# Linear attention: the third output tile moves from VectorE to ScalarE and GpSimd

## The reference, cut to what matters

```python
sq = elu_plus_one(q)                      # phi of the queries
sk = elu_plus_one(k)
kv = jnp.einsum('bhsd,bhse->bhde', sk, v)
qkv = jnp.einsum('bhsd,bhde->bhse', sq, kv)
k_sum = sk.sum(axis=2)
norm = jnp.einsum('bhsd,bhd->bhs', sq, k_sum)
attn = qkv / (norm[..., None] + EPS)
attn = attn.transpose(0, 2, 1, 3).reshape(b, s, H * D)
return attn @ Wo.T
...
x = x + _L0_attn_ref(_layernorm(x, axis=-1), ...)
```

## Time and profile before

| what | us |
|---|---|
| median of 3 runs | 3445.62 |
| lowest and highest | 3444.78, 3446.63 |
| the profiled execution | 3444.01 |
| its span | 3442.3 |

### The profile page before, as it was taken

The page is one execution under the profiler, slowest core; times in us unless marked ns, Lnnn a source line. Parts: engine busy times, 40 slices in busy tenths (PEclk is TensorE's granted clock), DMA queues, the critical chain, the costliest instruction groups (busy, mean ns, idle before and its releaser), DMA issues.

```text
span 3442.3 us, 53010 instructions
## 1 busy us (share of the span) xinstructions
PE 3337.5 (97%) x19523; PEld 2854.1 (83%) x19526; DVE 2670.2 (78%) x5148; ACT 2042.7 (59%) x3733; POOL 1062.4 (31%) x1295
## 2 busy tenths in 40 slices
PE   6899999999999999999999999999999999999997
PEld 4778888778888888888888888888888888888885
DVE  6899996778877788867788677886788767876776
ACT  4777777665556565555555656556555565556553
POOL 4887767622122122122121312212212121212112
PEclk9999999999999999999999999999999999999999
DMA  2221212200000000000000110001000010001000
GB/s 86 88 77 54 64 58 82 64 16 13 13 25 25 13 13 13 13 25 25 13 15 15 28 44 16 13 15 27 22 15 15 16 32 25 16 19 29 28 18 22
DMA packets 98528, 104.24 MB, mean 30 GB/s; under 512 B 10336, under 2 KB 88800, under 8 KB 98144
## 3 DMA queue, kind: packets, MB, share of 16 engines
q1 hardware_dynamic: 98272, 100.85, 9.8%
HBM read 87.18 MB, written 13.63 MB: 29 GB/s over the span
## 4 chain that ended last, share of the span: by engine, by line
PE 72%; DVE 5%; ACT 3%; DMA 0%; issue 0%; POOL 0%; DVEq 0%; ACTq 0%; POOLq 0%; SPq 0%
PE at_ps_job L2021 12%; PE at_ps_job L35 7%; PE at_ps_job L37 7%; PE at_ps_job L36 7%; PE at_ps_o L35 6%; PE at_ps_o L37 6%; PE at_ps_o L36 6%; PE at_ps_s L35 6%; PE at_ps_s L36 6%; PE at_ps_s L37 6%; DVE at_neg_max L1948 1%; ACT x_resident L1772 1%; DVE at_probT_lo L1815 1%; PE at_ps_job L656 1%; DVE li_wkv_lo L1846 0%; ACT at_probT_hi L1731 0%
## 5 line engine op out<-in xcount | busy, mean ns | idle before, releaser
L1731 ACT ACTIVATE at_probT_hi<-at_ps_job 128x512 fp32r<-128x512 f32 x1024 | 611.7, 598 | 888.3 <-PE at_ps_job L2021 885.7
L1815 DVE TENSOR_TENSOR at_probT_lo<-at_ps_job,at_probT_hi 128x512 fp32r<-128x512 f32 x1024 | 703.4, 687 | 272.7 <-ACT at_probT_hi L1731 262.4
L1772 ACT ACTIVATE x_resident<-at_ps_s,at_neg_max 128x1024 f32<-128x1024 f32 x512 | 570.9, 1115 | 150.6 <-DVE at_neg_max L1948 145.8
L1706 POOL TENSOR_TENSOR li_wkv_hi<-li_bkv,ch_cols 128x256 fp32r<-128x256 f32 x252 | 154.9, 615 | 1607.3 <-PE at_ps_job L37 1556.9
L1948 DVE TENSOR_REDUCE at_neg_max<-at_ps_s 128x1 f32<-128x1024 f32 x512 | 622.6, 1216 | 5.2
L2021 PE MATMUL at_ps_job<-ident,x_resident 128*128 128x128 f32 x4096 | 613.7, 272 | 4.7 <-DVE at_probT_lo L1815 2.9
L2021 PEld LDWEIGHTS at_ps_job<-ident,x_resident 128*128 128x128 f32 x4096 | 496.0, 140 | 97.4 <-issue 7.3
L35 PE MATMUL at_ps_o<-at_probT_hi,at_v_lo 128*128 128x512 f32 x1024 | 446.3, 436 | 7.6 <-DVE li_wkv_lo L1846 6.6
L35 PE MATMUL at_ps_s<-at_k_hi,at_q_lo 128*128 128x512 f32 x1024 | 445.1, 435 | 0.0
L37 PE MATMUL at_ps_o<-at_probT_lo,at_v_hi 128*128 128x512 f32 x1024 | 404.4, 395 | 0.0
L36 PE MATMUL at_ps_s<-at_k_hi,at_q_hi 128*128 128x512 f32 x1024 | 402.1, 393 | 0.0
(11 more groups left out here) (356 smaller groups left out, 7444.3 us busy)
## 6 DMA issues: line engine op xcount, KB each, us to landing
li_bkv<-attn_w SPq DMA_DIRECT2D x256, 128.0 KB, 2.3
li_bkv<-mlp_w SPq DMA_DIRECT2D x112, 128.0 KB, 2.3
li_wo_hi<-li_wo_kept SPq DMA_DIRECT2D x24, 256.0 KB, 2.7
li_wo_lo<-li_wo_kept SPq DMA_DIRECT2D x24, 256.0 KB, 3.0
li_wq_hi<-li_wq_kept SPq DMA_DIRECT2D x48, 128.0 KB, 2.1
li_wq_lo<-li_wq_kept SPq DMA_DIRECT2D x48, 128.0 KB, 2.3
x_resident<-x SPq DMA_DIRECT2D x4, 1024.0 KB, 14.3
out<-x_resident SPq DMA_DIRECT2D x4, 1024.0 KB, 4.9
```

Source lines behind the costliest of these rows:

```text
L1706: nc.gpsimd.tensor_tensor(hi, src, none, ALU.add).then_inc(s_wh[part], 1)
L1731: nc.scalar.activation(ph[:, i // TC, 4 * half:4 * half + 4, (i % TC) * P:(i % TC + 1) * P], c.turned_bank(2 * TB * u + 2 * i + half), ACT ...
L1772: nc.scalar.activation(prob[:, slot % 2, :], ps_s[slot % 2][:], ACT.Exp, bias=nmax[:, slot:slot + 1], accum_out=rsum[:, u % 2, slot:slot + ...
L1815: nc.vector.tensor_tensor(pl[at], c.turned_bank(2 * TB * u + 2 * i + half), ph[at].bitcast(F32), ALU.subtract).then_inc(s_pl, 1)
```

## The change

Each unit's third tile goes the way of the fourth. VectorE does two of the four tiles instead of three. ScalarE scales two tiles, one after the other, into two neighbouring parts of `ybuf`. GpSimd adds both to x in one operation of 512 columns instead of one of 256, and waits for both. The list of bank releases, and the three semaphore counts, follow.

```diff
@@ step_claims
-        for j in range(3):
-            yield ("OUT", m, j), "x", 3 * m + j + 1
-        yield ("OUT", m, 3), "y3", m + 1
+        for j in range(2):
+            yield ("OUT", m, j), "x", 2 * m + j + 1
+        for j in range(2):
+            yield ("OUT", m, 2 + j), "y23", 2 * m + j + 1
...
-        ybuf = sb("ybuf", [P, 2, D], F32)
+        ybuf = sb("ybuf", [P, 2, 2, D], F32)
...
@@ gpsimd
-                    pool.wait_ge(s_y3, m + 1)
-                    x = x_tile_of(m, 3)
-                    nc.gpsimd.tensor_tensor(x, ybuf[:, m % 2, :], x, ALU.add).then_inc(s_x3, 1)
+                    pool.wait_ge(s_y3, 2 * m + 2)
+                    x = x_tile_of(m, slice(2, 4))
+                    nc.gpsimd.tensor_tensor(x, ybuf[:, m % 2], x, ALU.add).then_inc(s_x3, 1)
...
@@ scalar
-                    nc.scalar.activation(ybuf[:, m % 2, :], c.own_bank(("OUT", m, 3))[:, 0:D], ACT.Copy,
-                                         scale=rnorm[:, m % 2, 3:4]).then_inc(s_y3, 1)
+                    for j in range(2):
+                        nc.scalar.activation(ybuf[:, m % 2, j, :], c.own_bank(("OUT", m, 2 + j))[:, 0:D], ACT.Copy,
+                                             scale=rnorm[:, m % 2, 2 + j:3 + j]).then_inc(s_y3, 1)
...
@@ vector
-                        dve.wait_ge(s_y3, m - 1)
-                        dve.wait_ge(s_x, 3 * m - 3)
+                        dve.wait_ge(s_y3, 2 * m - 2)
+                        dve.wait_ge(s_x, 2 * m - 2)
...
-                    for j in range(3):
+                    for j in range(2):
                         x = x_tile_of(m, j)
                         nc.vector.scalar_tensor_tensor(x, c.own_bank(("OUT", m, j))[:, 0:D], rnorm[:, m % 2, j:j + 1], x, ALU.mult, ALU.add).then_inc(s_x, 1)
```

More of the change, by code:

```diff
@@ L1019, in linear_attention_phase @@
         aw = AttentionWeights(kv)
-        c.own_emptied = {"phi": s_f, "x": s_x, "y3": s_y3}
+        c.own_emptied = {"phi": s_f, "x": s_x, "y23": s_y3}
         block = ctx.enter_context(nc.Block())
@@ L1038, in x_tile_of @@
         def x_tile_of(m, j):
-            return sh.x[:, m // LOOP * TB + m % 2 * TC + j, :]
+            x = sh.x[:, m // LOOP * TB + m % 2 * TC:m // LOOP * TB + m % 2 * TC + TC, :]
+            return x[:, j, :]
         def ready(dve, kind, b):
@@ L1046, in ready @@
             if kind == "QB":
-                dve.wait_ge(s_x, 3 * LOOP)
+                dve.wait_ge(s_x, 2 * LOOP)
                 dve.wait_ge(s_x3, LOOP)
```

## The result

| | median us | lowest, highest | profiled span |
|---|---|---|---|
| before | 3445.2 | 3444.72, 3446.63 | 3442.3 |
| after | 3476.3 | 3474.48, 3479.55 | 3475.4 |

The ratio after to before is 1.0091, with a 95% interval of 1.0080 to 1.0103: 31 us slower, where 8.8 us faster was forecast and 3449 was the end of the range.

A forecast was written before the change was run, and what follows sets the result against it. Linear attention was taken as bound by VectorE's list in some stretches and TensorE in the others. Terms -12.7 - 2.5 + 3.0 + 2.5 + 0.9 = -8.8 us, forecast 3436.8 us (profiled 3435.2); range 3426 to 3449.

The forecast's parts named there:

- Where the time is bound: Linear attention: VectorE's list bounds some stretches, TensorE the others; 30.8 us of TensorE's stalls end with VectorE's `f`.
- Relief, -12.7: VectorE in linear attention: one tile fewer, net 0.30 us a step where VectorE is late; -12.7 us, bounds -30.8 and -1.7.
- clock, -2.5: TensorE's slower products after four of the stalls: about half of this goes; -2.5 us, bounds 0 and -5.6.
- The stretching, +0.10 us a step: VectorE's SBUF instructions beside GpSimd's longer addition: 27 x 0.49 = 13 us come back, 0.10 us a step.
- the 43 steps: Steps where VectorE's relief was counted: 29 in four long stretches, 14 or so in shorter ones.
- the four long stretches: Windows before TensorE's larger stalls, 6, 5, 6 and 12 steps, VectorE never idle; 21.5 us of TensorE's idle time.
- GpSimd's late list, +3.0: 174 to 218 us: nine wider additions make GpSimd's list late, TensorE waits for phi's low part; +3.0 us, bounds 0 and +4.8.
- the predicted stretch: 174 to 218 us, GpSimd busy 43.25 of 44.0 us, its list 3.7 us late at the end.
- ScalarE's second scaling, +2.5: ScalarE, 345 to 367 us and four shorter places: +0.42 us a step delays phi's high part; +2.5 us, bounds 0 and +6.
- The end, +0.9: End of linear attention, before the barrier: scaling 0.42 and addition 0.49 longer with nothing beside them; +0.9 us.
- The slower one: Rival, first 30 steps: GpSimd's list becomes the bound, stretching takes the whole relief; +9 us, 3455, chance 0.13.
- Q: Theory of the follow-up experiments, not the prediction: GpSimd's list runs late and TensorE waits for phi's low part.

The follow-up runs named there:

- e1: Changed kernel with the third tile left out: VectorE adds two tiles, ScalarE scales one, GpSimd adds 256 columns; 3436.5 us, ratio to before 0.9974.
- e2: Changed kernel without the third tile's scaling on ScalarE; GpSimd still adds 512 columns, half of them zeros; 3468.6 us.
- e4: Kernel before, with ScalarE scaling a tile a second time into a spare buffer ahead of the real scaling; 3456.6 us.
- e3: Changed kernel with ScalarE's two scalings, but GpSimd adds only the fourth tile (256 columns); 3444.6 us.
- e13: Kernel before, with four tiles on VectorE in units 16 to 55, 64 to 79 and 104 to 111, old division elsewhere; 3441.1 us, ratio 0.9989.
- e14: Kernel before, with four tiles on VectorE in units 0 to 15, 56 to 63, 80 to 103 and 112 to 127; 3449.7 us, ratio 1.0012.
- e9: Kernel before, with all four tiles on VectorE, no scaling on ScalarE and no addition on GpSimd; 3445.2 us, ratio 0.9999.

## Why the prediction was wrong

**Where the time is bound: right.** TensorE's idle time came from `f`, `f` from VectorE's arrears, and with the relief alone (e1) TensorE's waits for `f` fell from 30.8 to 25.3 us and the time by 9 us.

**Relief, -12.7 and clock, -2.5: too large.** Together they gave -9.2 in e1. Up to the barrier, TensorE's idle time fell by 5.9 us there and its busy time by 3.4; it ran at the lower clock level for 15 us instead of 17, so the clock's share is small and not measured by itself. A part of the relief turned into a new wait: VectorE's next step begins with evictions that wait for ScalarE, and shorter tiles only bring it there sooner. `DVE li_m_lo <- ACT li_m_hi` was 3.7 us in the whole phase before, and 16.1 us in 32 waits in e1. The prediction never looked at what VectorE does right behind its tiles.

**The stretching, +0.10 us a step inside the relief term: the step that failed.** The prediction counted 27 stretched instructions that span the end of an addition and gave each 0.49 us: 13 us. It then multiplied the 0.10 us a step only by the 43 steps in which VectorE was taken as the bound, so that 4.3 us entered the sum. Measured were 26 to 30 us more stretching (before to after, 15 of the 30 in L104 and L1335, where some 10 were forecast) and 32 us more time. Two things were wrong.

The smaller one is the count over the old trace, in which new meetings can't be seen. Sorted by the GpSimd operation that they end behind, 31 instructions with 11.3 us of stretching belonged to the addition before, and 40 with 35.3 us after. The 31, each 0.52 us longer, are 16 us, near the 13 counted. Nine more that now fall beside the longer addition are 8. The other 5 lie behind other operations; the closed gap in the rows of e2 is of this kind. The bound of 46 us (all 93 instructions) was in the text.

The larger one is that stretching was taken to cost nothing outside those 43 steps. In the trace of before, 30 of the 61 us of stretching begin outside the four long stretches. From e1 to e2 the 31 units that fall in these stretches lost 16.6 us and all others 13.5. So outside the stretches, too, VectorE had less room than the prediction took it to have. Nearly the whole stretching became time, not the 43 steps' share of it.

**GpSimd's late list, +3.0: of the right kind, small beside the other.** TensorE waits for phi's low part at four places, 3.4 us in all, the largest at the end of the predicted stretch (which lies some 10 us later in this trace):

```profile
229.16 0.39 PE L35 MATMUL li_ps<-li_m_hi,li_phi_lo 128*128 128x258 f32 x1 [1.56 <-POOL li_phi_lo L1157]
```

**ScalarE's second scaling, +2.5: too small.** It cost 8 us, 11 in e4. The prediction weighed it against ScalarE's idle time at the end of the step and found four places. It left out that the evictions behind it are waited for by VectorE: `DVE li_m_lo <- ACT li_m_hi` went from 16.1 (e1) to 21.7 us (e3), and VectorE's wait for Exp from 6.8 to 10.4. This account is argued, not shown: in e4, with a cost of 11 us, the same two waits grew by 6.6 us only.

**The end, +0.9: right.** The chain after the change:

```profile
704.07 0.84 ACT L1262 ACTIVATE li_ybuf<-li_ps,li_rnorm 128x256 f32<-128x256 f32 x2 [2.01 <-DVE li_rnorm L1350]
...
704.98 1.26 POOL L1163 TENSOR_TENSOR x_resident<-li_ybuf,x_resident 128x512 f32<-128x512 f32 x1 [0.79 <-ACT li_ybuf L1262]
...
707.78 0.59 PE L35 MATMUL at_ps_job<-ch_xnT_hi,li_wkv_lo 128*128 128x512 f32 x1 [4.29 <-PEq L81]
```

TensorE stands idle 4.29 us at the barrier, against 3.39 in the earlier trace rows.

**The rivals.** The slower one had the right engine and named stretching as what takes the relief, but saw its place in the first 30 steps and its price at +9 to +10. Measured from e1 to e2, units 0 to 31 cost 10 us and the other 96 twice that. The rule of the GPSIMD Engine Reference of the Trainium skill that GpSimd is about twice as slow at elementwise operations with two inputs (section 4.1, Engine selection) pointed to this rival. The rows gave less than that, 0.54 us for the tile against VectorE's 0.40, and the addition's own length was not the trouble.

**What stays open.** How much of the 32 us is Q's. How the second scaling comes to cost 8 to 11 us. Why e13 and e14 reach only 0.55 and 0.75 of what e9's units promised.

## What to carry to other kernels

Work that moves to GpSimd in SBUF is paid for by VectorE as well, if VectorE's list holds instructions of the kinds that were seen to wait here: those with two SBUF inputs, and `TENSOR_SCALAR` from SBUF to SBUF. Look in the trace for instructions far over the shortest of their kind, and count what a longer GpSimd operation will newly meet, also in steps where VectorE is not the bound yet. Here 0.54 us of it cost 0.25 us a step, and moving 0.40 us of PSUM-reading work off VectorE gained 0.07. Before work is taken off an engine, look at the first wait behind it: the engine may only arrive there sooner.

## What the runs showed of the hardware

- Some of VectorE's instructions waited for GpSimd's: of 127 in the phase after the change that took at least 0.1 us over their shortest, all ended a fixed time after a GpSimd operation (L104 0.15 us, L1338 0.28 us). L588 took 0.43 us with GpSimd idle and 1.45 beside it, L91, with 8 columns, up to 1.33.
- Others did not wait: statistics with one SBUF input (L528, 128x256) took 397 to 420 ns in the kernel after, the additions that read PSUM (L1360) 472 to 484.
- GpSimd's addition took 0.26 us for 8 columns, 0.80 for 256 and 1.35 for 512, and its price in the kernel's time grew from 13 us for the first of these steps to 32 us for the second.
- With all four tiles on VectorE (e9) the kernel stayed where it was: 51 us more additions on VectorE against 24 us less stretching, 53 us less ScalarE and 98 us less GpSimd time.
